# The order of plain score units between the other TensorE work in an attention stage

## The chip, the cores and the metric

The kernel runs on one core of a Trainium2 chip. The metric is device time of one execution in microseconds. Before the change the median of three runs is 2106.28 us (2105.14 to 2108.61).

## The reference

One transformer layer in fp32 over 2048 positions of width 512: x + attention(xn) + feed-forward(xn), where xn is x normalised over its last axis. Cut to what matters here:

```python
qkv = einsum('bsh,oh->bso', xn, w_qkv)      # 16 heads of 32
scores = einsum('bhqd,bhkd->bhqk', q, k) / sqrt(32)
scores = where(causal, scores, finfo.min)
probs = softmax(scores, axis=-1)
attn = einsum('bhqk,bhkd->bhqd', probs, v)
out = einsum('bsh,oh->bso', attn, w_o)
```

The feed-forward (512 to 4096 and back, weights unpacked from 4-bit codes) is not touched.

## The kernel before

There are three stages, each with one program for each engine and semaphores between them: norm_and_project, attention, project_and_feed_forward. The change is in the attention's TensorE program.

The attention computes each head's scores twice. The first time, the *plain score units* give the row maxima: `scores` (L628 to L638) multiplies 128 query rows by up to 512 keys into p_s, a PSUM tile with two buffers, and adds the causal mask to units on the diagonal with a second small matmul. VectorE's `unit_max` reduces each unit to one column of max_part (L533). A head has 40 units. They go through the query blocks 0 to 15 in order, each cut into chunks of 512 keys, so that the last unit of a block has 128, 256, 384 or 512 columns and a mask. `scores` waits until VectorE has reduced the unit two before (L629): maxed starts at 2.

`split_max` (L536 to L553) then splits a head's maxima into three bf16 parts. `turn_max` (L640 to L650) transposes them by matmul into p_o, ScalarE's `max_row` copies them into spare rows of q_stack, in four pieces of 512 columns a head.

The second time, `scores_t` (L652 to L668) computes transposed scores with the maximum already subtracted, in 20 *steps* a head. A step is 256 keys by 512 query columns (256 in the last step of each query chunk). The chunks have 2, 4, 6 and 8 steps; the last two of each carry masks. ScalarE takes the exponential (L490), and `product_v` (L670 to L683) multiplies it by v into p_o: two concurrent halves, which go to different partitions. At the end of a chunk ScalarE copies one half (`copy_half`), and VectorE's `add_halves` (L555 to L563, two operations of 512 columns) adds the halves and frees p_o.

TensorE's order is written out in `group` (L710 to L727), a loop over *pairs* of steps (d from 0 to 9). In a pair the transposed scores run two steps ahead of the products. The plain units of later heads are spread over the steps, two to each: BESIDE[s] (L294 to L297) holds units 10 to 39 of the next head in steps 0 to 14 and units 0 to 9 of the one after in steps 15 to 19. The order of a pair is: two units, scores_t of two steps, turn_max (pairs 8 and 9), two units, product_v of two steps, turn_max (pairs 8 and 9). The loop over groups of four heads jumps back twice; the last group is written out, and leaves out units of heads that don't exist.

VectorE's order is written in its own `group` (L601 to L617): for each step its two unit_max, and behind those of steps 3, 7 and 13 the add_halves of the chunk that ended two steps earlier; the last chunk's stands at the head's end. In step 15 split_max comes ahead of the units. Each engine takes its instructions in this order.

In the pairs the units have these columns (d for a mask): pair 0 512, 512d, 512, 512; pair 1 128d, 512, 512, 256d; pair 2 512, 512, 384d, 512; pair 3 512, 512d, 512, 512; pair 4 512, 128d, 512, 512; pair 5 512, 256d, 512, 512; pair 6 512, 384d, 512, 512; pair 7 512, 512d, 128d, 256d; pair 8 384d, 512d, 512, 128d; pair 9 512, 256d, 512, 384d..

Of the kernel before, what the change touches and what calls it, by code (L numbers as in the profile page):

```python
# [262 lines left out]
def attention(nc, qk_scratch, v_scratch, sum_scratch, rsum_scratch, wo_t, wo_sb, attn_t):  # L263
# [11 lines left out]
    GROUP = 4  # L275
# [3 lines left out]
    QK_BUFS = GROUP  # L279
# [3 lines left out]
    LEAD = 2  # L283
# [10 lines left out]
    BESIDE = {s: [] for s in range(NS)}  # L294
# [12 lines left out]
    with ExitStack() as ctx:  # L307
# [3 lines left out]
        def sem(name):  # L311
            return ctx.enter_context(nc.semaphore(name))
# [25 lines left out]
        qk_loaded = [sem(f"qk_loaded{i}") for i in range(QK_BUFS)]  # L338
# [107 lines left out]
        def ahead(g, j, s, steps, last):  # L446

            dj, s = divmod(s + steps, NS)
            if last and j + dj >= GROUP:
                return None  # L450
            return g * GROUP + j + dj, (j + dj) % GROUP, s
# [171 lines left out]
        @block.tensor  # L623
        def _(pe):
            pe.sem_inc(pv_done, E_BUFS)
            pe.wait_ge(consts, NC + 3)

            def scores(h, par, u):  # L628

                i, k, w = UNITS[u]  # L630
                diagonal = k + w == P * (i + 1)
                pe.wait_ge(maxed, h * NU + u + 1)
                last = nc.tensor.matmul(p_s[:, u % 2, 0:w], q_stack[par][0:ROWS, i * P:(i + 1) * P],  # L633
                                        k_stack[par][0:ROWS, k:k + w], start=True, stop=not diagonal)
                if diagonal:
                    last = nc.tensor.matmul(p_s[:, u % 2, w - P:w], ident[:, :], mask_q[:, :],
                                            start=False, stop=True)
                last.then_inc(scored, 1)  # L638

            def turn_max(h, r):  # L640

                if r == 0:
                    pe.wait_ge(max_split, h + 1)
                    pe.wait_ge(o_free, h * TC + 1)
                    pe.wait_ge(denom_made, h * TC + 1)
                pe.wait_ge(max_rows, h * TC + r + 1)
                for t in range(W // P):
                    last = nc.tensor.matmul(p_o[:, 0, t * P:(t + 1) * P], max_cols[:, r * (W // P) + t, :],
                                            ident[:, :], start=True, stop=True)
                last.then_inc(max_turned, 1)  # L650

            def scores_t(h, par, s):  # L652

                qc, pair, q0 = STEPS[s]
                w = W - q0
                if pair == 0:
                    pe.wait_ge(max_rows, h * TC + qc + 2)
                pe.wait_ge(exp_done, h * NS + s + 1)
                for t in range(2):
                    kt = 2 * pair + t  # L660
                    diagonal = kt * P >= qc * W
                    last = nc.tensor.matmul(p_st[:, s % 2, t, 0:w], k_stack[par][:, kt * P:(kt + 1) * P],  # L662
                                            q_stack[par][:, qc * W + q0:(qc + 1) * W], start=True,
                                            stop=not diagonal)
                    if diagonal:
                        last = nc.tensor.matmul(p_st[:, s % 2, t, 0:(t + 1) * P], ident[:, :],
                                                mask_k[:, (1 - t) * P:], start=False, stop=True)
                last.then_inc(st_ready, 1)  # L668

            def product_v(h, par, s):  # L670
                qc, pair, q0 = STEPS[s]
                w = W - q0
                if pair == 0:
                    pe.wait_ge(o_free, h * TC + qc + 1)
                    pe.wait_ge(denom_made, h * TC + qc + 1)
                if s == 0:
                    pe.wait_ge(max_rows, (h + 1) * TC + 1)
                pe.wait_ge(exp_done, h * NS + s + 3)
                for t in range(2):
                    last = nc.tensor.matmul(p_o[2 * t * D:2 * t * D + VW, qc % 2, q0:], v_stack[par][:, 2 * pair + t, :],  # L680
                                            e_sb[:, s % E_BUFS, t, 0:w], start=pair == 0, stop=s in LAST)
                last.then_inc(pv_done, 1)

            pe.sem_inc(maxed, 2)
            pe.sem_inc(max_rows, 1)
            for u in range(NU):
                if u == 0:
                    pe.wait_ge(qk_loaded[0], 96)
                scores(0, 0, u)
            for r in range(TC):  # L690
                turn_max(0, r)
            pe.wait_ge(minus_one, 2 * QK_BUFS + V_BUFS)
            for s in range(LEAD):
                scores_t(0, 0, s)
            for s in range(CHAIN, NS):
                for heads, u in BESIDE[s]:
                    if u == 0:
                        pe.wait_ge(qk_loaded[heads - 1], 96)
                    scores(heads - 1, heads - 1, u)

            def scores_beside(g, j, s, last):
                for heads, u in BESIDE[s]:
                    if last and j + heads >= GROUP:
                        continue
                    par = (j + heads) % QK_BUFS
                    if u == 0:
                        pe.wait_ge(qk_loaded[par], (g + (j + heads) // QK_BUFS + 1) * 96)
                    scores(g * GROUP + j + heads, par, u)

            def group(g, last):  # L710
                for j in range(GROUP):
                    h = g * GROUP + j
                    turns = not (last and j + 1 >= GROUP)
                    pe.wait_ge(v_loaded[j % V_BUFS], (g * (GROUP // V_BUFS) + j // V_BUFS + 1) * 16)
                    for d in range(ND):
                        s = 2 * d
                        scores_beside(g, j, s, last)
                        for n in (s, s + 1):
                            if (at := ahead(g, j, n, LEAD, last)) is not None:
                                scores_t(*at)  # L720
                        if turns and d >= ND - 2:
                            turn_max(h + 1, 2 * (d - ND + 2))
                        scores_beside(g, j, s + 1, last)
                        product_v(h, j % V_BUFS, s)
                        product_v(h, j % V_BUFS, s + 1)
                        if turns and d >= ND - 2:
                            turn_max(h + 1, 1 + 2 * (d - ND + 2))  # L727

            with pe.Fori(0, NH // GROUP - 1) as g:
                group(g, False)  # L730
            group(NH // GROUP - 1, True)


# [391 lines left out]
```

## Time and profile before

| | |
|---|---|
| median of 3 runs | 2106.28 us |
| profiled execution | 2107.61 us, span 2105.8 us, mean granted clock 0.969 |
| TensorE busy, matmuls | 1958.8 us (93%) |
| VectorE busy | 1197.6 us (57%) |
| ScalarE busy | 706.9 us (34%) |
| GpSimd busy | 239.1 us (11%) |
| attention | from about 200 to 944 us |
| feed-forward | from about 962 us to the end |

The span goes from the first to the last instruction of one profiled execution. An engine's busy time leaves out its waits. Matmuls are pipelined and their recorded ends are modelled, so that the record of one outlasts the start of the next. PEld stands for TensorE's weight loads, which run beside its matmuls. The granted clock is TensorE's: 1.00 is 2.4 GHz, 0.50 is 1.2 GHz. What is named behind "idle before" is what ended that idle time.

### The profile page before, as it was taken

To read this page: it belongs to the slowest core of one execution; us is meant where nothing else is said; L and a number is where in the kernel's file an instruction comes from. 1 tells how busy PE (TensorE), PEld (TensorE's weight loads), DVE (VectorE), ACT (ScalarE), POOL (GpSimd) and SP (SyncE) were. 2 spreads that over 40 slices of the span, in tenths; PEclk is the share of its full clock that TensorE was granted. 3 is DMA by queue.
4 is the path that set the end of the run, shared out by engine and by line. 5 is a ranking of instruction groups with operands and counts; after the bars stand their busy time and mean duration, and the time that the engine had idled before them with its cause. 6 is when DMAs were issued, how large, how long until landed. Compare 5 with 4: busy or idle time off the path is not lost.

```text
span 2105.8 us, 25238 instructions
## 1 busy us (share of the span) xinstructions
PE 1958.8 (93%) x8704; PEld 1337.9 (64%) x8704; DVE 1197.6 (57%) x1645; ACT 706.9 (34%) x825; POOL 239.1 (11%) x153
## 2 busy tenths in 40 slices
PE   2997899989999999987999999999999999999998
PEld 2885444444444444433777877788777877778776
DVE  7211666666667666665355655555655655656543
ACT  2221254544555545550123232222232222222221
POOL 0003000000000000000112122111122121111121
PEclk9998699999999999998999999999999999999999
DMA  3755211123111121305211011100110011110002
GB/s 140 247 173 145 65 36 36 36 39 67 37 37 36 36 56 23 68 20 191 60 31 31 0 30 30 30 23 7 30 30 30 0 30 30 30 27 3 0 1 80
DMA packets 84862, 106.29 MB, mean 50 GB/s; under 512 B 41680, under 2 KB 58256, under 8 KB 80976
## 3 DMA queue, kind: packets, MB, share of 16 engines
q1 hardware_dynamic: 84784, 105.27, 18.8%
q8 instruction: 47, 0.77, 0.2%
q14 instruction: 31, 0.25, 0.0%
HBM read 75.62 MB, written 29.61 MB: 50 GB/s over the span
## 4 chain that ended last, share of the span: by engine, by line
DVE 21%; ACT 11%; POOL 10%; issue 6%; PE 6%; POOLq 0%; DVEq 0%; ACTq 0%
POOL poly L923 7%; DVE acc L996 5%; DVE inter L976 4%; DVE inter L980 4%; ACT inter L895 3%; POOL poly L920 3%; ACT gate L891 3%; ACT poly L892 3%; DVE weight L965 3%; ACT i_hi L898 2%; DVE pair L952 2%; DVE magnitude L959 2%; PE p_out L1061 1%; DVE high L956 1%; DVE pair L950 1%
## 5 line engine op out<-in xcount | busy, mean ns | idle before, releaser
L533 DVE TENSOR_REDUCE max_part<-p_s 128x1 f32<-128x512 f32 (+3 forms) x640 | 364.2, 606 | 255.7 <-PE p_s L633 144.1
L490 ACT ACTIVATE e_sb<-p_st 128x1024 f32<-128x1024 f32 x320 | 282.8, 935 | 248.8 <-PE p_st L662 146.9
L680 PE MATMUL p_o<-e_sb,v_stack 128*33 128x512 f32 (+1 forms) x1280 | 292.1, 579 | 3.5 <-DVE acc L558 3.5
L633 PE MATMUL p_s<-k_stack,q_stack 96*128 96x512 f32 (+3 forms) x640 | 241.5, 445 | 50.2 <-DVE max_part L533 29.7
L976 DVE SCALAR_TENSOR_TENSOR inter<-inter,gate 128x1024 f32<-128x1024 f32 x64 | 78.4, 1226 | 329.4 <-ACT inter L895 329.4
L920 POOL TENSOR_SCALAR poly<-poly 128x1024 f32<-128x1024 f32 x64 | 67.4, 1053 | 1649.4 <-ACT poly L892 1649.4
L633 PEld LDWEIGHTS p_s<-k_stack,q_stack 96*128 96x128 f32 x640 | 115.4, 202 | 177.7 <-DVE max_part L533 131.7
L48 PE MATMUL p_up<-xn_hi,w_hi 128*128 128x512 f32 x512 | 201.0, 393 | 25.4 <-DVE inter L980 25.4
L48 PE MATMUL p_out<-i_hi,w_hi 128*128 128x512 f32 x512 | 200.0, 391 | 3.1 <-DVE acc L996 3.1
L48 PE MATMUL p_gate<-xn_hi,w_hi 128*128 128x512 f32 x512 | 201.5, 394 | 0.6 <-ACT poly L892 0.6
L662 PE MATMUL p_st<-q_stack,k_stack 128*128 128x512 f32 (+1 forms) x640 | 200.6, 422 | 0.0
L49 PE MATMUL p_out<-i_lo,w_hi 128*128 128x512 f32 x512 | 199.9, 391 | 0.0
L50 PE MATMUL p_out<-i_hi,w_lo 128*128 128x512 f32 x512 | 199.7, 390 | 0.0
L49 PE MATMUL p_gate<-xn_lo,w_hi 128*128 128x512 f32 x512 | 199.4, 389 | 0.0
L49 PE MATMUL p_up<-xn_lo,w_hi 128*128 128x512 f32 x512 | 199.4, 389 | 0.0
L50 PE MATMUL p_up<-xn_hi,w_lo 128*128 128x512 f32 x512 | 199.4, 389 | 0.0
L50 PE MATMUL p_gate<-xn_hi,w_lo 128*128 128x512 f32 x512 | 199.3, 389 | 0.0
L885 ACT ACTIVATE w_hi<-weight 128x1024 fp32r<-128x1024 f32 x48 | 50.9, 1061 | 393.1 <-DVE weight L965 393.1
L680 PEld LDWEIGHTS p_o<-e_sb,v_stack 128*33 128x33 f32 x1280 | 63.1, 113 | 143.9 <-issue 107.2
L923 POOL TENSOR_TENSOR poly<-poly,gate 128x1024 f32<-128x1024 f32 x64 | 153.2, 2393 | 5.3
L996 DVE TENSOR_TENSOR acc<-acc,p_out 128x2048 f32<-128x2048 f32 x64 | 145.9, 2280 | 7.5 <-PE p_out L50 7.5
L895 ACT ACTIVATE inter<-poly 128x1024 f32<-128x1024 f32 x64 | 67.9, 1061 | 240.5 <-POOL poly L923 240.5
(105 smaller groups left out, 2623.0 us busy)
## 6 DMA issues: line engine op xcount, KB each, us to landing
q_stack<-qk_scratch SPq DMA_DIRECT2D x48, 256.0 KB, 4.3
k_stack<-qk_scratch SPq DMA_DIRECT2D x48, 256.0 KB, 6.7
qk_scratch<-out_hi SPq DMA_DIRECT2D x32, 256.0 KB, 2.6
qk_scratch<-out_lo SPq DMA_DIRECT2D x32, 256.0 KB, 3.3
scales<-in_gate_up_s SPq DMA_DIRECT2D x128, 64.0 KB, 2.3
x_sb<-in_x SPq DMA_DIRECT2D x4, 1024.0 KB, 12.0
xn_lo_scratch<-xn_lo_made SPq DMA_DIRECT2D x1, 4096.0 KB, 13.3
v_scratch<-out_v SPq DMA_DIRECT2D x16, 256.0 KB, 2.0
```

The costliest lines, as they stand in the source:

```text
L48: nc.tensor.matmul(out, w_hi, x_hi, start=first, stop=False)
L49: nc.tensor.matmul(out, w_hi, x_lo, start=False, stop=False)
L50: return nc.tensor.matmul(out, w_lo, x_hi, start=False, stop=last)
L490: nc.scalar.activation(e_sb[:, s % E_BUFS, :, 0:w], p_st[:, s % 2, :, 0:w], ACT.Exp, scale=SCALE).then_inc(exp_done, 1)
L533: nc.vector.reduce_max(max_part[:, i, k // CAP:k // CAP + 1], p_s[:, u % 2, 0:w], AX.X).then_inc(maxed, 1)
L633: last = nc.tensor.matmul(p_s[:, u % 2, 0:w], q_stack[par][0:ROWS, i * P:(i + 1) * P], k_stack[par][0:ROWS, k:k + w], start=True, stop=not ...
L662: last = nc.tensor.matmul(p_st[:, s % 2, t, 0:w], k_stack[par][:, kt * P:(kt + 1) * P], q_stack[par][:, qc * W + q0:(qc + 1) * W], start=True,
L680: last = nc.tensor.matmul(p_o[2 * t * D:2 * t * D + VW, qc % 2, q0:], v_stack[par][:, 2 * pair + t, :], e_sb[:, s % E_BUFS, t, 0:w], start ...
L895: nc.scalar.activation(inter[:, :, :], poly[:, :, :], ACT.Tanh, scale=GELU_B).then_inc(tanh_done, 1)
L923: nc.gpsimd.tensor_tensor(poly[:, :, :], poly[:, :, :], gate[:, :, :], ALU.mult).then_inc(poly_done, 1)
L976: nc.vector.scalar_tensor_tensor(inter[:, :, :], inter[:, :, :], 1.0, gate[:, :, :], ALU.add, ALU.mult).then_inc(gelu_done, 1)
L996: nc.vector.tensor_tensor(here, here, p_out[:, :, :], ALU.add).then_inc(added, 1)
```

## The change

The four plain units of a pair no longer stand two by two. scores_beside places one unit, and is called four times in a pair. The new order of a pair is: unit, scores_t of one step, unit, scores_t of the other step, turn_max (pairs 8 and 9), unit, product_v of two steps, turn_max (pairs 8 and 9), unit. Only TensorE's program changes.

```diff
--- before.py
+++ after.py
@@ -698,14 +698,18 @@
                         pe.wait_ge(qk_loaded[heads - 1], 96)
                     scores(heads - 1, heads - 1, u)
 
-            def scores_beside(g, j, s, last):
-                for heads, u in BESIDE[s]:
-                    if last and j + heads >= GROUP:
-                        continue
-                    par = (j + heads) % QK_BUFS
-                    if u == 0:
-                        pe.wait_ge(qk_loaded[par], (g + (j + heads) // QK_BUFS + 1) * 96)
-                    scores(g * GROUP + j + heads, par, u)
+            def scores_beside(g, j, s, last, which):
+                heads, u = BESIDE[s][which]
+                if last and j + heads >= GROUP:
+                    return
+                par = (j + heads) % QK_BUFS
+                if u == 0:
+                    pe.wait_ge(qk_loaded[par], (g + (j + heads) // QK_BUFS + 1) * 96)
+                scores(g * GROUP + j + heads, par, u)
+
+            def scores_t_ahead(g, j, s, last):
+                if (at := ahead(g, j, s, LEAD, last)) is not None:
+                    scores_t(*at)
 
             def group(g, last):
                 for j in range(GROUP):
@@ -714,17 +718,18 @@
                     pe.wait_ge(v_loaded[j % V_BUFS], (g * (GROUP // V_BUFS) + j // V_BUFS + 1) * 16)
                     for d in range(ND):
                         s = 2 * d
-                        scores_beside(g, j, s, last)
-                        for n in (s, s + 1):
-                            if (at := ahead(g, j, n, LEAD, last)) is not None:
-                                scores_t(*at)
+                        scores_beside(g, j, s, last, 0)
+                        scores_t_ahead(g, j, s, last)
+                        scores_beside(g, j, s, last, 1)
+                        scores_t_ahead(g, j, s + 1, last)
                         if turns and d >= ND - 2:
                             turn_max(h + 1, 2 * (d - ND + 2))
-                        scores_beside(g, j, s + 1, last)
+                        scores_beside(g, j, s + 1, last, 0)
                         product_v(h, j % V_BUFS, s)
                         product_v(h, j % V_BUFS, s + 1)
                         if turns and d >= ND - 2:
                             turn_max(h + 1, 1 + 2 * (d - ND + 2))
+                        scores_beside(g, j, s + 1, last, 1)
 
             with pe.Fori(0, NH // GROUP - 1) as g:
                 group(g, False)
```

## Rows read from the trace of the kernel before

**Rows 1.** Busy time by stage: stretch, its length, each engine, granted clock, DMA.

```profile
250.00:944.00 694.00, 657.22 (x3218) 304.88 (x3214) 456.99 (x825) 350.33 (x439) 0.00 (x0) 0.96 0.20 40
```

**Rows 2.** Waits in the attention: who for whom, us in all, times, longest.

```profile
PEld p_s L633 <- DVE max_part L533: 116.3, 165, 2.4
...
PE p_s L633 <- DVE max_part L533: 26.0, 25, 2.0
```

**Rows 3.** Busy time by stage, head 7: pairs 1 to 5, 7 and 9.

```profile
566.09:570.17 4.08, 4.08 (x23) 1.90 (x23) 2.93 (x6) 2.10 (x3) 0.00 (x0) 1.00 1.00 204
570.17:573.92 3.75, 3.75 (x18) 1.90 (x18) 2.92 (x5) 1.94 (x2) 0.00 (x0) 1.00 0.58 56
573.92:578.08 4.16, 4.16 (x18) 1.75 (x18) 3.42 (x6) 2.53 (x3) 0.00 (x0) 1.00 0.00 0
578.08:582.22 4.14, 4.14 (x22) 1.83 (x22) 2.72 (x5) 1.51 (x2) 0.00 (x0) 1.00 0.00 0
582.22:585.71 3.49, 3.49 (x18) 1.75 (x18) 2.31 (x4) 1.94 (x2) 0.00 (x0) 1.00 0.00 0
...
589.73:594.05 4.32, 4.15 (x20) 1.94 (x20) 3.63 (x11) 1.94 (x2) 0.00 (x0) 1.00 0.01 2
...
598.60:602.84 4.24, 4.24 (x32) 2.38 (x32) 2.18 (x4) 2.69 (x4) 0.00 (x0) 1.00 0.00 0
```

**Rows 4.** Timeline of TensorE, head 7, pair 3: start, us, instructions, idle before.

```profile
572.42 1.49 PE L680 MATMUL p_o<-e_sb,v_stack 128*33 128x512 f32 x8
573.83 0.73 PE L633 MATMUL p_s<-k_stack,q_stack 96*128 96x512 f32 x2
...
574.45 1.17 PE L662 MATMUL p_st<-q_stack,k_stack 128*128 128x512 f32 x4
...
576.14 1.91 PE L680 MATMUL p_o<-e_sb,v_stack 128*33 128x512 f32 x8
```

**Rows 5.** Timeline of VectorE, head 7, pair 3.

```profile
574.37 1.29 DVE L533 TENSOR_REDUCE max_part<-p_s 128x1 f32<-128x512 f32 x2 [1.15 <-PE p_s L633]
...
577.21 0.69 DVE L558 TENSOR_TENSOR acc<-p_o,half_sum 32x512 f32 x1
...
578.65 0.89 DVE L533 TENSOR_REDUCE max_part<-p_s 128x1 f32<-128x512 f32 x2
```

**Rows 6.** Groups of VectorE in the attention: busy us, mean ns, idle before.

```profile
L533 DVE TENSOR_REDUCE max_part<-p_s 128x1 f32<-128x512 f32 x413 | 272.9, 687 | 141.0 <-PE p_s L633 135.7 <-PE p_s L636 3.4
...
L533 DVE TENSOR_REDUCE max_part<-p_s 128x1 f32<-128x256 f32 x58 | 24.0, 414 | 0.0
```

**Rows 7.** Timelines of VectorE and TensorE where heads 6 and 7 meet.

```profile
559.78 0.69 DVE L558 TENSOR_TENSOR acc<-p_o,half_sum 32x512 f32 x1 [2.18 <-ACT half_sum L497]
...
561.22 1.97 DVE L533 TENSOR_REDUCE max_part<-p_s 128x1 f32<-128x512 f32 x3
...
561.97 1.39 PE L633 MATMUL p_s<-k_stack,q_stack 96*128 96x512 f32 x2 [2.00 <-DVE max_part L533]
```

**Rows 8.** Timeline of the weight loads, head 7, pairs 2, 3 and 0.

```profile
571.99 0.19 PEld L633 LDWEIGHTS p_s<-k_stack,q_stack 96*128 96x128 f32 x1
...
575.71 0.19 PEld L633 LDWEIGHTS p_s<-k_stack,q_stack 96*128 96x128 f32 x1 [0.31 <-DVE max_part L533]
...
562.56 0.29 PEld L633 LDWEIGHTS p_s<-k_stack,q_stack 96*128 96x128 f32 x1 [0.41 <-DVE max_part L533]
```

**Rows 9.** Timeline of TensorE at a loop jump, between heads 3 and 4.

```profile
424.65 0.73 PE L633 MATMUL p_s<-k_stack,q_stack 96*128 96x512 f32 x2 [3.07 <-issue]
```

**Rows 10.** Busy time by stage, pairs 0 and 1 together, of heads 1 and 9.

```profile
287.08:299.14 12.06, 9.97 (x44) 4.54 (x43) 6.89 (x12) 5.12 (x7) 0.00 (x0) 0.86 0.61 138
...
648.21:658.70 10.49, 8.40 (x44) 3.84 (x44) 6.89 (x12) 5.13 (x7) 0.00 (x0) 1.00 0.57 133
```

**Rows 11.** Timeline of TensorE and busy time by stage in the feed-forward.

```profile
1152.86 0.50 PE L48 MATMUL p_up<-xn_hi,w_hi 128*128 128x512 f32 x1 [1.60 <-DVE inter L980]
...
1064.00:2027.00 963.00, 938.52 (x4108) 768.45 (x4106) 562.27 (x573) 270.64 (x271) 196.44 (x114) 1.00 0.08 21
```

## The prediction

> **What bounds the kernel now.** I read the stages first. In the attention's stretch TensorE (PE) is busy 657.2 of 694.0 us, VectorE (DVE) 457.0 and ScalarE 350.3 [rows 1]: TensorE sets the pace, and a stall there costs its full length. The change touches only TensorE's order in this stretch, so the rest of the program keeps its time.
>
> The waits come second. In this stretch weight loads of the plain score units wait on VectorE's row maxima 165 times, 116.3 us in all; the score matmuls themselves only 25 times, 26.0 us [rows 2]. Most waits of a load are thus covered by matmuls still streaming, and few reach the array. What they hang on is p_s, with two buffers: unit n can't start before VectorE has reduced unit n-2.
>
> Third, one head pair by pair (a pair is one d, two steps). I call the units of a pair U0 to U3, their reductions r0 to r3, the transposed scores T and T', the products V. Head 7's pairs 1 to 5, 7 and 9 take 4.08, 3.75, 4.16, 4.14, 3.49, 4.32 and 4.24 us at full clock [rows 3]. Pair 0, where the heads meet, is the exception, below.
>
> **The queue behind the change.** Before, a pair is U0 U1 T T' U2 U3 V. After, it is U0 T U1 T' U2 V U3. Nothing is added or removed: the same matmuls, loads and waits. But VectorE's order stays as written: r0 r1 r2 r3, and after steps 3, 7 and 13 the additions of a finished chunk (add_halves, two operations) stand between r3 of pair 1, 3, 6 and r0 of the next pair. Before, U3 ran ahead of the products, so r3 and the additions ran under them. After, U3 runs behind the products, so r3 and the additions begin only when the next pair's U0 is already through; r0 comes behind them, and U2 of that pair waits for r0.
>
> **Term 1, U2 behind the additions.** The pair's time from the end of the previous products:
> - The first unit behind the products starts at 573.83, and its reduction at 574.37, 0.46 us after the products' end at 573.91 (572.42 + 1.49) [rows 4, 5]. So r3 starts at 0.46 and, at 0.69 for 512 columns (687 ns on average), ends at 1.15; for U3 of 256 columns (pair 1) it takes 0.41 and, the unit being shorter, ends at 0.85 [rows 5, 6].
> - The additions and the gaps around them: from 577.21 to the next reduction at 578.65 is 1.44 us, plus 0.03 ahead of them [rows 5]. r0 thus starts at 2.62 and ends at 3.31 (pair 1's follower: 2.32, 3.01).
> - A waiting unit starts 0.06 after a reduction (561.22 + 0.69 = 561.91, and 561.97), its load some 0.01 earlier [rows 7]. So U2 loads at 3.36 (3.06).
> - From the load of the last unit ahead of the products to their end: 575.71 to 578.05 = 2.34 us, and 571.99 to 573.91 = 1.92 where half of the products are 256 wide [rows 4, 8].
> - Pair 4 becomes 3.36 + 2.34 = 5.70 against 4.14: +1.56. Pair 2 becomes 3.06 + 1.92 + 0.03 for a masked unit = 5.01 against 3.75: +1.26. Pair 7's U2 has 128 columns, some 0.10 less: 5.60 against 4.32: +1.28 [rows 3].
>
> Units stand beside heads 0 to 14; in head 14 pair 7 has no U2. The term: 15 x 1.26 + 15 x 1.56 + 14 x 1.28 = 18.9 + 23.4 + 17.9 = 60.2 us. What hid the additions until now was 1.9 us of products; that cover is gone. The bounds: nothing, if r0 weren't behind the additions, and 44 x 1.99 = 88 us, the length of the one stall of this kind that the trace has, where the heads meet [rows 7].
>
> **Term 2, the U1 that follows U3 closely.** U3, U0 and T now stand ahead of U1, and U1 needs r3: it loads at 1.20 at the earliest. Until U2's load come U1 (0.25) and T' (0.50: T and T' last from 574.45 to 575.45 [rows 4]), and from there it is 2.34: pair 3 takes 4.29, with the mask matmul of its U1 4.31, against 4.16 [rows 3]. Before, the U3 of this pair waited for r1 instead (its load at 575.71, 0.31 idle [rows 8]): the wait moves rather than goes. By the same sum, with each pair's own widths, pair 1 grows by 0.20, pair 3 by 0.15, pair 5 by 0.29 and pair 6 by 0.24; pair 9 shrinks by 0.16, as its masked U3 of 384 columns moves on and a short one comes, and pair 8 by 0.02. Together 15 x 0.88 - 14 x 0.18 = +10.7 us. The bounds: 0 where T covers r3 after all, 20 if every U1 waits 0.4.
>
> **Term 3, where the heads meet.** The last additions wait for ScalarE's copy (559.78, idle 2.18 us before), the next reduction starts at 561.22, and U2 stands still for 2.00 us; U3's load follows at 562.56, 0.60 behind, again for a reduction [rows 7, 8]. ScalarE's copy comes at the same time after the change, r0 too; U2 keeps its release, but U3 now stands behind the products. So 0.60 us go at each of the 12 boundaries that have units and no loop jump: -7.2 us. At the two loop jumps TensorE waits 3.07 us on its own issue and r0 is ready by then [rows 9]: nothing. The visible idle time before U2 shrinks from 2.00 to 1.74, as U3 and its masks fill 0.26.
>
> **Term 4, the clock.** Ten of these 12 boundaries are followed by a spell at the lower clock level (1.2 instead of 2.4 GHz): pairs 0 and 1 take 12.06 us at a mean clock of 0.86 against 10.49 where the clock stays [rows 10], so 1.6 us a spell. What precedes it is 2.00 us of idle [rows 7]. In the feed-forward TensorE idles 1.60 us at a time for VectorE's line L980, and the clock stays at 1.00 over 963 us [rows 11]. The idle of term 1's stalls starts when T' is through. U3 starts at -0.08; U3, U0, U1 take 0.25 each, T and T' 0.50 each, masks up to 0.3, and a record outlasts the next start by 0.17 (574.45 + 1.17 = 575.62) [rows 4]: 1.84 to 2.15. To 3.36 (pair 2: 3.06) these are 1.2 to 1.5 us, below 1.60: I take no new spell. The boundaries' 1.74 lies between the rows: I take half of the ten spells as gone, -8.0 us; the bounds are 0 and -16.
>
> The Trainium skill speaks against this, in its page "TensorE: Matmul & The Clock Gate", section "A second HAM failure mode: psum-queue depth-cycling": where the engine idles briefly and often between groups of matmuls over rotating PSUM buffers, its clock swings between the two levels, and throughput goes down by that. The feed-forward's rows don't bear it out; the heads' boundaries do. By the rule all 44 new stalls would be followed by a spell: the first rival.
>
> **Sum.** 60.2 + 10.7 - 7.2 - 8.0 = +55.7 us on the profiled execution's own 2107.6 (span 2105.8): 2163.3. The median before is 2106.3, 1.3 lower: I predict 2162 us, 2.6% slower.
>
> **Rivals.**
> 1. *Every new stall costs a spell too.* For it: the attention's stretch is less dense than the feed-forward (657.2 of 694.0 against 938.5 of 963.0 us busy), so a shorter idle may do [rows 1, 11]. Against: idle of 1.60 never did. 44 x 1.6 = 70 and the 8 of term 4 not gained: 2240. 15%; a part of the stalls (a third) gives 2193.
> 2. *Only term 1 and 3 show.* T covers r3, and all ten spells go: 60.2 - 7.2 - 16 = +37: 2143. For it: 0.4 us is within what loads wait today without the array idling [rows 2]. Against: pair 3's U3 waits in just this way and pays. 10%.
> 3. *Faster.* One mechanism: spacing. With a piece of other work between any two units, no unit of a pair waits for the reduction that just began; the 26.0 us of matmul waits [rows 2] and the ten spells, 16 us, would go: 2064. It decides at the U2 that follows the additions: if VectorE has r0 done when T' ends, it holds. It would need some 1.3 us of slack in VectorE's queue just where U3 now comes 2 us later. 4%.
> 4. *It does nothing*, the waits only change places: 2106. Term 2 shows that for the ordinary pairs; the additions' place speaks against it for the others. 3%.
>
> The forecast itself has 68%. Its own range is 2150 to 2175; the range to hold 8 in 10 reaches down to rival 2 and up past a third of rival 1: 2142 to 2205. About 0.2% (4 us) can be told from no change in this kernel. Faster 4%, same 3%, slower 93%.
>
> **What would show it.** In the profile after, the idle before the score matmuls caused by VectorE's reductions grows from 26 us by some 55, in about 44 more waits of 1.3 to 1.5 us; pairs 2, 4 and 7 of head 7 take 5.0, 5.7 and 5.6 us, the others change by less than 0.35; VectorE's additions start about 1.2 us after the products' end and not under them; fewer rows at 0.86 where heads meet. I am wrong if the stall before U2 is missing or much shorter than 1.2 us, or if pairs 2, 4 and 7 carry a clock below 1.00.

## The result and the profile after

The changed kernel takes 2170.18 us at the median (2168.28 to 2171.04, 4 runs) against 2107.45 for the kernel before in the same comparison: a ratio of 1.0296, interval 1.0278 to 1.0314. Forecast were 2162 us, range 2142 to 2205. The profiled execution has 2168.28 us and a span of 2166.5, 60.7 above the span before.

The instructions are the same in number (25238). What has grown is idle time. The waits first, in the attention's stretch, now 250 to 1001 us: the columns are those of [rows 2].

```profile
PEld p_s L633 <- DVE max_part L533: 129.0, 145, 2.0
...
PE p_s L633 <- DVE max_part L533: 71.1, 58, 1.5
```

The score matmuls wait 58 times and 71.1 us on VectorE's reductions, where it was 25 times and 26.0 [rows 2]. The 58 are the 44 stalls of term 1, 12 where heads meet and 2 others; the 25 were 12 of 1.9 to 2.0 us and 13 small ones. The growth is 45 us and not 55: the idle in a stall is 1.07 to 1.23 us and not 1.3 to 1.5, as T' ends later than I summed, and where heads meet the idle fell from 2.00 to 1.52 us. The loads' waits have become fewer, 145 for 165. So it isn't the number of waits that decides, but how many reach the array.

Head 7 pair by pair, the busy time by stage as in [rows 3], all ten pairs:

```profile
584.05:589.87 5.82, 4.30 (x23) 1.96 (x23) 3.91 (x6) 3.05 (x4) 0.00 (x0) 1.00 0.19 55
589.87:594.14 4.27, 4.27 (x22) 1.89 (x22) 2.27 (x4) 2.11 (x3) 0.00 (x0) 1.00 1.03 226
594.14:599.15 5.01, 3.82 (x19) 1.86 (x19) 3.65 (x6) 1.94 (x2) 0.00 (x0) 1.00 0.83 113
599.15:603.52 4.37, 4.29 (x18) 1.75 (x18) 2.67 (x4) 2.65 (x3) 0.00 (x0) 1.00 0.00 0
603.52:609.25 5.73, 4.50 (x22) 2.04 (x22) 3.65 (x6) 1.51 (x2) 0.00 (x0) 1.00 0.00 0
609.25:613.08 3.83, 3.74 (x18) 1.75 (x18) 2.35 (x4) 2.05 (x2) 0.00 (x0) 1.00 0.00 0
613.08:617.40 4.32, 4.23 (x18) 1.75 (x18) 2.54 (x4) 2.64 (x3) 0.00 (x0) 1.00 0.00 0
617.40:623.02 5.62, 4.47 (x19) 1.83 (x19) 4.76 (x12) 2.05 (x2) 0.00 (x0) 1.00 0.02 5
623.02:627.67 4.65, 4.65 (x29) 2.28 (x30) 2.27 (x4) 2.10 (x3) 0.00 (x0) 1.00 0.00 0
627.67:631.85 4.18, 4.18 (x32) 2.35 (x33) 2.10 (x4) 2.69 (x4) 0.00 (x0) 1.00 0.00 0
```

Pairs 2, 4 and 7 (third, fifth and eighth row) take 5.01, 5.73 and 5.62 us against 3.75, 4.14 and 4.32 [rows 3]; forecast were 5.0, 5.7 and 5.6. In pair 2 only 3.82 of the 5.01 us are busy. All ten rows have a clock of 1.00. Pair 0 took 8.00 us before, in the spell (558.09 to 566.09), and takes 5.82.

Pairs 3 and 4 on VectorE, answering to [rows 5]:

```profile
599.59 2.80 DVE L533 TENSOR_REDUCE max_part<-p_s 128x1 f32<-128x512 f32 x4 [1.29 <-PE p_s L633]
603.96 0.69 DVE L533 TENSOR_REDUCE max_part<-p_s 128x1 f32<-128x512 f32 x1 [1.58 <-PE p_s L633]
604.68 0.69 DVE L558 TENSOR_TENSOR acc<-p_o,half_sum 32x512 f32 x1
605.41 0.69 DVE L562 TENSOR_TENSOR denom<-p_o,half_sum 1x512 f32<-1x512 f32 x1
606.13 0.89 DVE L533 TENSOR_REDUCE max_part<-p_s 128x1 f32<-128x512 f32 x2
```

The products of pair 3 end at 603.50, r3 starts at 603.96 as forecast (0.46 behind), the additions at 604.68, and r0 at 606.13. Under the products of pair 3, from 602.4 to 603.96, VectorE now has nothing to do. TensorE in pair 4:

```profile
601.59 1.91 PE L680 MATMUL p_o<-e_sb,v_stack 128*33 128x512 f32 x8
603.43 0.73 PE L633 MATMUL p_s<-k_stack,q_stack 96*128 96x512 f32 x2
...
604.92 0.36 PE L662 MATMUL p_st<-q_stack,k_stack 128*128 128x256 f32 x1
...
606.87 0.51 PE L633 MATMUL p_s<-k_stack,q_stack 96*128 96x512 f32 x1 [1.23 <-DVE max_part L533]
607.31 1.91 PE L680 MATMUL p_o<-e_sb,v_stack 128*33 128x512 f32 x8
```

T' starts at 604.92. U2 starts at 606.87 after 1.23 us of idle, 0.05 behind the end of r0 (606.13 + 0.69 = 606.82).

### The profile page after: what moved, and what is told of

Same layout as the page of the kernel before. It is cut to its first block, busy times and chain, and to the rows that moved or that the text cites. A ratio compares the mean times of both kernels' runs of the same rounds, so it can differ in the third digit from the quotient of the medians.

```text
span 2166.5 us, 25238 instructions
## 1 busy us (share of the span) xinstructions
PE 1967.7 (91%) x8704; PEld 1333.7 (62%) x8704; DVE 1210.1 (56%) x1645; ACT 714.7 (33%) x825; POOL 239.2 (11%) x153
## 4 chain that ended last, share of the span: by engine, by line
DVE 20%; ACT 11%; POOL 10%; issue 6%; PE 6%; POOLq 0%; DVEq 0%; ACTq 0%
POOL poly L928 7%; DVE acc L1001 5%; DVE inter L981 3%; DVE inter L985 3%; ACT inter L900 3%; POOL poly L925 3%; ACT gate L896 3%; ACT poly L897 3%; DVE weight L970 3%; ACT i_hi L903 2%; DVE magnitude L964 1%; DVE pair L957 1%; PE p_out L1066 1%; DVE high L961 1%; PE p_gate L1066 1%
## 5 line engine op out<-in xcount | busy, mean ns | idle before, releaser
L533 DVE TENSOR_REDUCE max_part<-p_s 128x1 f32<-128x512 f32 (+3 forms) x640 | 376.7, 609 | 327.7 <-PE p_s L633 174.8
L490 ACT ACTIVATE e_sb<-p_st 128x1024 f32<-128x1024 f32 x320 | 290.1, 937 | 291.5 <-PE p_st L662 169.3
L633 PE MATMUL p_s<-k_stack,q_stack 96*128 96x512 f32 (+3 forms) x640 | 266.8, 455 | 99.6 <-DVE max_part L533 75.3
L680 PE MATMUL p_o<-e_sb,v_stack 128*33 128x512 f32 (+1 forms) x1280 | 283.7, 565 | 3.2 <-DVE acc L558 3.2
L633 PEld LDWEIGHTS p_s<-k_stack,q_stack 96*128 96x128 f32 x640 | 119.9, 199 | 252.4 <-DVE max_part L533 144.5
L662 PE MATMUL p_st<-q_stack,k_stack 128*128 128x512 f32 (+1 forms) x640 | 217.9, 415 | 0.0
```

Of the source, the lines that this page charges most:

```text
L490: nc.scalar.activation(e_sb[:, s % E_BUFS, :, 0:w], p_st[:, s % 2, :, 0:w], ACT.Exp, scale=SCALE).then_inc(exp_done, 1)
L533: nc.vector.reduce_max(max_part[:, i, k // CAP:k // CAP + 1], p_s[:, u % 2, 0:w], AX.X).then_inc(maxed, 1)
```

## The experiments

In all of them the letters are those of the prediction. The kernel before, run beside each comparison, had 2107.21 and 2107.9 us at the median. Times by pair are those of head 7; in the kernels before and after the change heads 1 to 11 agree with it to 0.03 us in pairs 2 to 9.

### The halves of the change, one at a time

U0 and U1 are spaced, and U3 stays ahead of the products:

```diff
-scores_beside(g, j, s + 1, last, 0)
-product_v(h, j % V_BUFS, s)
+scores_beside(g, j, s + 1, last, 0)
+scores_beside(g, j, s + 1, last, 1)
+product_v(h, j % V_BUFS, s)
 ...
-scores_beside(g, j, s + 1, last, 1)
```

> Only the first half of the change: U0 T U1 T' U2 U3 V; U3 stays ahead of the products. My theory (the cost is U3 behind the products, with the additions between its reduction and the next pair's): no stall behind the additions, the 44 waits of 1.1 to 1.2 us are missing; r1 comes some 0.07 us later for U3 in the pairs whose U1 has 512 columns; the boundaries stay as before with their 0.60 and their spells. Time: before plus 2 to 8 us, 2110 to 2115. The rival (units one by one are dearer as such, by the array's switching between plain and transposed units): half of the +61 us, some 2135.

Measured: 2115.41 us (2111.28 to 2120.53), ratio 1.0045 (1.0029 to 1.0061). The pairs behind the additions keep their old times. Busy time by stage, pairs 1, 3, 4 and 7 of head 7:

```profile
565.57:569.98 4.41, 4.34 (x23) 1.97 (x23) 3.28 (x6) 2.10 (x3) 0.00 (x0) 1.00 1.03 223
573.81:578.15 4.34, 4.30 (x18) 1.76 (x18) 3.69 (x6) 2.53 (x3) 0.00 (x0) 1.00 0.00 0
578.15:582.28 4.13, 4.13 (x22) 1.80 (x22) 2.64 (x5) 1.51 (x2) 0.00 (x0) 1.00 0.00 0
589.95:594.24 4.29, 4.16 (x20) 1.95 (x20) 3.62 (x11) 1.94 (x2) 0.00 (x0) 1.00 0.01 2
```

Pair 4 takes 4.13 and pair 7 4.29 us. The stalls are not there. Pair 3 takes 4.34 against 4.16, pair 1 4.41 against 4.08: U1 comes 0.5 to 0.7 us later than beside U0, r1 with it, and U3, still close behind, pays. The 8 us lie at the upper edge of what I gave (2 to 8) and are an eighth of the change's cost; the rival's 2135 is out. They are a net sum: in the profiled execution pairs 1 to 9 grew by 11 us over heads 0 to 14, spells left out, and four of the ten spells were missing.

The other half alone: U0 and U1 side by side, U3 behind the products.

```diff
 scores_beside(g, j, s, last, 0)
-scores_t_ahead(g, j, s, last)
 scores_beside(g, j, s, last, 1)
+scores_t_ahead(g, j, s, last)
 scores_t_ahead(g, j, s + 1, last)
```

> Only the second half of the change: U0 U1 T T' U2 V U3. My theory: the three stalls behind the additions are there in full (60 us), and U1, now only U0 behind U3, waits for r3 with nothing but U0 in between: its load at 1.20 us, with T and T' both still to come. By the sum from the ends of reductions pairs 1, 3, 5, 6, 8, 9 are 0.3 to 0.7 us longer than in the changed kernel, together 2.7 us a head, 40 us: about 2210 us. The rival (spacing is the dear part): 2140, the other half of the +61.

Measured: 2209.44 us, ratio 1.0492 (1.0473 to 1.0511). Busy time by stage, pairs 2, 3 and 4:

```profile
617.32:622.32 5.00, 4.02 (x19) 1.92 (x19) 3.66 (x6) 1.94 (x2) 0.00 (x0) 1.00 0.70 87
622.32:627.15 4.83, 4.28 (x18) 1.74 (x18) 2.67 (x4) 2.53 (x3) 0.00 (x0) 1.00 0.00 0
627.15:632.87 5.72, 4.66 (x22) 1.95 (x22) 3.66 (x6) 1.51 (x2) 0.00 (x0) 1.00 0.00 0
```

That is my theory's 2210, and not the rival's 2140. Pairs 2 and 4 stall as in the changed kernel (5.00, 5.72), and pair 3 takes 4.83 where that has 4.37. So with U3 behind the products the spacing of U0 and U1 is worth 39 us, and with U3 ahead of them it costs 8. The halves can't be added: +8 and +102 alone, +63 together.

### Where VectorE's additions stand

TensorE's order stays that of the change; only VectorE's moves. First the additions go between r2 and r3:

```diff
-for heads, u in BESIDE[s]:
+for n, (heads, u) in enumerate(BESIDE[s]):
     ...
-if s - 2 in LAST:
-    add_halves(g, h, j, STEPS[s - 2][0])
+    if n == 0 and s - 2 in LAST:
+        add_halves(g, h, j, STEPS[s - 2][0])
```

> TensorE's order as in the changed kernel; on VectorE the additions of a chunk stand between r2 and r3 instead of behind r3, so that they run under the products again. My theory: pairs 2, 4 and 7 fall from 5.00, 5.72 and 5.62 to about 3.5, 4.1 and 4.2 us, 66 us in all: 2100 to 2106, at or slightly below the kernel before, because the boundaries keep their gain. The rival (U3 behind the products is dear by itself, whatever VectorE's order): it stays above 2140.

Measured: 2105.74 us (12 runs), ratio 0.9995 (0.9986 to 1.0005): no difference from the kernel before, and 64 us below the changed one. VectorE's timeline in pairs 3 and 4, and then the busy time by stage of pairs 2, 4 and 7:

```profile
569.94 0.69 DVE L558 TENSOR_TENSOR acc<-p_o,half_sum 32x512 f32 x1
570.66 0.69 DVE L562 TENSOR_TENSOR denom<-p_o,half_sum 1x512 f32<-1x512 f32 x1
571.48 1.49 DVE L533 TENSOR_REDUCE max_part<-p_s 128x1 f32<-128x512 f32 x3
```

```profile
563.13:566.67 3.54, 3.54 (x19) 1.85 (x19) 2.58 (x5) 1.94 (x2) 0.00 (x0) 1.00 0.75 70
571.04:575.27 4.23, 4.23 (x22) 1.96 (x22) 2.49 (x5) 1.51 (x2) 0.00 (x0) 1.00 0.00 0
583.45:587.72 4.27, 4.19 (x19) 1.84 (x19) 3.69 (x11) 2.05 (x2) 0.00 (x0) 1.00 0.03 6
```

The additions now start at 569.94, under the products that end at 571.02, and pairs 2, 4 and 7 take 3.54, 4.23 and 4.27 us. Over all heads these three pairs give back 63 us; the others keep the times of the changed kernel. This is the strongest evidence: nothing on TensorE has changed against the slow kernel. That the time draws level with the kernel before is a balance, of what the other pairs cost more and what the shorter waits where heads meet save.

Then one place later than in the changed kernel, between r0 and r1 (the condition is n == 0 and s - 3 in LAST):

> TensorE's order as in the changed kernel; on VectorE the additions stand one place later, between r0 and r1 of the next pair. My theory (only r0 behind the additions is dear): U2 of pairs 2, 4 and 7 finds r0 at 1.75 us and doesn't stall; r1 ends about 3.8, needed by U3 only behind the products at about 4.1; 2103 to 2112. The rival (the additions need the products' cover, anywhere else they cost 1.44 us each time, 44 x 1.44 = 63 us): about 2165.

Measured: 2129.81 us, ratio 1.0103 (1.0086 to 1.0121), outside what either theory gave. Pairs 2 and 4 are mended (3.54, 4.23). Pair 8 is not. VectorE's timeline from pair 7 on, TensorE's, and the busy time by stage of pairs 3 and 8:

```profile
598.61 0.69 DVE L558 TENSOR_TENSOR acc<-p_o,half_sum 32x512 f32 x1
...
600.05 0.69 DVE L533 TENSOR_REDUCE max_part<-p_s 128x1 f32<-128x512 f32 x1
...
602.15 0.62 DVE L533 TENSOR_REDUCE max_part<-p_s 128x1 f32<-128x128 f32 x2
```

```profile
602.50 0.44 PE L633 MATMUL p_s<-k_stack,q_stack 96*128 96x384 f32 x1 [1.01 <-DVE max_part L533]
```

```profile
579.88:584.46 4.58, 4.47 (x18) 1.85 (x18) 3.19 (x6) 2.55 (x3) 0.00 (x0) 1.00 0.03 4
601.13:607.01 5.88, 4.87 (x29) 2.35 (x30) 3.45 (x10) 2.10 (x3) 0.00 (x0) 1.00 0.00 0
```

Ahead of pair 7's r2 now stand the additions, r1 and split_max. r2 starts at 602.15, and U0 of pair 8, which needs its buffer, starts at 602.50 after 1.01 us of idle. Pair 8 takes 5.88 us for 4.65. In pair 3 a smaller wait of this kind shows (4.58 for 4.37). Moved work needs slack for every unit that the new place delays. I had looked at r0 and r1 only.

### The heads' boundaries, and a faster kernel

TensorE's order of the kernel before; the last chunk's additions of a head go behind r3 of the next head's pair 0:

```diff
 if s - 2 in LAST:
     add_halves(g, h, j, STEPS[s - 2][0])
-add_halves(g, h, j, TC - 1)
+        if s == 1 and j > 0:
+            add_halves(g, h - 1, j - 1, TC - 1)
+if j == GROUP - 1:
+    add_halves(g, h, j, TC - 1)
```

> TensorE's order of the kernel before; on VectorE the last chunk's additions of a head stand behind r3 of the next head's pair 0 instead of ahead of its r0, for all heads but the last of a group. My theory (a stall is r0 behind additions, here too, and the spell follows the stall): the 2.0 us and 0.60 us waits go at 11 boundaries with units, pair 0 falls from 6.35 to about 3.95 us, and with the idle goes the spell: 11 x 2.4 + 9 x 1.6 = 40 us: 2062 to 2072. The rival (the wait at the boundary is for ScalarE's turned maxima and copies, and moves to the products): 2100 to 2107.

Measured: 2069.37 us (2067.54 to 2071.41), ratio 0.9816 (0.9803 to 0.983), faster than both kernels and within what my theory gave; the rival's 2100 is out. Pairs 0 and 1, and then pair 0 in the kernel before, of heads 7 (in a spell) and 9:

```profile
537.67:541.57 3.90, 3.90 (x22) 1.93 (x21) 3.01 (x5) 3.02 (x4) 0.00 (x0) 1.00 0.00 0
541.57:545.86 4.29, 4.29 (x23) 1.99 (x23) 3.99 (x8) 2.10 (x3) 0.00 (x0) 1.00 0.41 100
```

```profile
558.09:566.09 8.00, 5.91 (x22) 2.22 (x22) 4.04 (x6) 3.02 (x4) 0.00 (x0) 0.79 0.43 102
648.21:654.61 6.40, 4.31 (x22) 1.93 (x22) 3.95 (x6) 3.02 (x4) 0.00 (x0) 1.00 0.31 78
```

Pair 0 takes 3.90 us at full clock where it took 8.00, or 6.40 without a spell.

The same with the changed TensorE order, all additions between r2 and r3:

> TensorE's order as in the changed kernel; all additions between r2 and r3, and the last chunk's in the next head's pair 0. My theory: as with the additions ahead of r3 alone (2106), less 11 boundaries of some 1.6 us and the spells left there (5 x 1.6): 2078 to 2090, behind the kernel before with its boundary mended by the price of U1 behind U3, 17 us. A rival (one by one is the better order once VectorE's is right): below 2065.

Measured: 2087.42 us, ratio 0.9903 (0.9888 to 0.9918), as my theory had it and 18 us above the kernel just shown. With VectorE's additions moved for either, one by one remains the dearer order.

Last, U3 between the products of the two steps. VectorE's order is that of the run just shown, and the edit is against that run:

```diff
 product_v(h, j % V_BUFS, s)
+scores_beside(g, j, s + 1, last, 1)
 product_v(h, j % V_BUFS, s + 1)
 ...
-scores_beside(g, j, s + 1, last, 1)
```

> The order U0 T U1 T' U2 V U3 V', U3 between the products of the two steps, with all additions between r2 and r3, the last chunk's in the next head's pair 0. My theory: r3 has half of the products as cover, so U1 no longer waits for it, and nothing waits for the additions: pair 3 about 4.1 us, pair 5 3.5, pair 6 4.0, pair 2 3.6: 2055 to 2068, some 5 us below the kernel before with its boundary mended. The rival: each piece more between products costs about 0.1 us in loads and fills, and it ends level with that kernel or above it, to 2080.

Measured: 2109.73 us, ratio 1.0006 (0.9997 to 1.0015). My theory fell, and by more than its rival allowed. TensorE's timeline in pair 3, and the busy time by stage of pairs 3 and 4:

```profile
572.18 1.05 PE L683 MATMUL p_o<-e_sb,v_stack 128*33 128x512 f32 x4
573.16 0.49 PE L636 MATMUL p_s<-k_stack,q_stack 96*128 96x512 f32 x1
573.59 1.05 PE L683 MATMUL p_o<-e_sb,v_stack 128*33 128x512 f32 x4
574.57 0.51 PE L636 MATMUL p_s<-k_stack,q_stack 96*128 96x512 f32 x1
```

```profile
570.31:574.66 4.35, 4.35 (x18) 1.66 (x18) 3.81 (x7) 2.53 (x3) 0.00 (x0) 1.00 0.63 59
574.66:579.12 4.46, 4.46 (x22) 1.79 (x22) 2.82 (x5) 1.51 (x2) 0.00 (x0) 1.00 0.00 0
```

No wait shows in these rows, so U1 indeed no longer waits for r3. But pair 4 takes 4.46 us for 4.14. In pair 3 U3 and the products of both steps last from 572.18 to 574.57, 2.39 us. In the changed kernel the products of both steps last 1.84 us in one piece (601.59 to 603.43). Here each step's take 0.98, 0.12 more for the two, and U3 takes 0.43, where a unit in the forecast's sum had 0.25: 0.3 us a pair for the place between the products.

Against the run before, where U3's place is the only difference, pairs 2, 4, 8 and 9 are longer by 0.28, 0.22, 0.23 and 0.38 us; in pairs 3, 5 and 6 the wait that is gone just pays for it (0.01 to 0.03 shorter), and pair 7 is 0.07 shorter. Together with pairs 0 and 1 that makes 22 us over heads 0 to 14, of which longer spells ahead of heads 4, 8 and 12, where the additions still stand at a group's end, are about 7. With the 18 us by which that run lies above the kernel with its boundary mended, this takes back the 38 us that mending the boundary brought. The theory saw what is saved and put the place between the products at nothing.

### Longer stalls: what the clock does

The changed kernel, with one more VectorE operation between the additions of chunks 0 to 2:

```diff
 nc.vector.tensor_tensor(attn_t[...], p_o[...], half_sum[...], ALU.add)
+if qc < TC - 1:
+    nc.vector.tensor_tensor(idle_work, half_sum[...], half_sum[...], ALU.add)
 nc.vector.tensor_tensor(denom[...], p_o[...], half_sum[...], ALU.add)
```

> The changed kernel, with one more VectorE operation of 512 columns (half_sum added to itself into an unused tile) between the two additions of chunks 0 to 2; the output doesn't depend on it. My theory: each of the 44 stalls is longer by 0.72 us, 31.7 us in all, and the idle in them is 1.8 to 1.95 us. If the clock falls after idle of that length, as it did where heads met, most of the 44 are followed by a spell of 1.6 us: up to 70 us more, 2240 to 2270. The rival (the spells at the boundaries are due to what surrounds them, not to the idle's length): plus 32 only, 2202, and no row below 1.00 in pairs 2, 4 and 7.

Measured: 2226.67 us, ratio 1.0559 (1.054 to 1.0578), 56.5 above the changed kernel and between the two theories (2240 and up; 2202). The operation and its gap take 0.70 us on VectorE, 44 times, 30.8 us. The rest goes with the clock. Busy time by stage of head 7's pairs 2, 4 and 7, and TensorE's timeline in pair 7:

```profile
620.79:626.81 6.02, 4.12 (x19) 1.84 (x19) 4.34 (x7) 1.94 (x2) 0.00 (x0) 0.93 0.68 96
632.05:640.10 8.05, 6.13 (x22) 2.22 (x22) 4.34 (x7) 1.51 (x2) 0.00 (x0) 0.79 0.00 0
648.26:655.68 7.42, 5.57 (x19) 1.90 (x19) 5.45 (x13) 2.05 (x2) 0.00 (x0) 0.84 0.00 0
```

```profile
652.31 0.33 PE L636 MATMUL p_s<-k_stack,q_stack 96*128 96x128 f32 x1 [1.78 <-DVE max_part L534]
...
652.64 3.02 PE L683 MATMUL p_o<-e_sb,v_stack 128*33 128x512 f32 x8
```

After idle of 1.78 us the products take 3.02 us for 1.91, and the mean clock of this pair is 0.84. Of the 44 stalls 21 are followed by a spell. In the two profiled executions pairs 2 to 9 of heads 0 to 14 grew by 61.4 us (head 13's pair 3 left out, where a spell went); less 30.8 that is 30.6, or 1.5 us a spell. Both theories had a part: length does bring spells, but at 1.65 to 1.92 us only to about half of the stalls. Counted in one profiled execution of each kernel, idle of the array in the attention and spells at the lower clock behind it:

| kernel and place | idle, us | spells |
|---|---|---|
| additions behind r0, pair 8 | 1.00 to 1.02 | 0 of 12 |
| second half, boundaries | 0.95 to 1.07, behind one of some 0.4 | 1 of 12 |
| changed, pairs 2, 4 and 7 | 1.07 to 1.23 | 0 of 44 |
| head 13's pair 3, in four of the kernels | 1.23 to 1.25 | 2 of 4 |
| changed, boundaries | 1.41 to 1.53 | 1 of 12 |
| additions ahead of r3, boundaries | 1.41 to 1.53 | 2 of 12 |
| additions behind r0, boundaries | 1.41 to 1.53 | 5 of 12 |
| longer stalls, boundaries | 1.41 to 1.53 | 0 of 12 |
| longer stalls, pairs 2, 4 and 7 | 1.65 to 1.92 | 21 of 44 |
| first half, boundaries | 1.87 to 1.99 | 6 of 12 |
| before, boundaries | 1.89 to 2.00 | 10 of 12 |

The counts belong to these executions and not to the kernels. The twelve executions of the kernel with the additions ahead of r3 go from 2103.1 us at a mean granted clock of 0.977 to 2109.4 us at 0.973, so some of them had more or longer spells than the one counted (2103.8 us). A difference of a few spells between two rows shows nothing; that of 0 of 44 against 21 of 44 does.

## Why the prediction was right, step by step

**Term 1** (60.2 us) is right in place and size. Over heads 0 to 14 pairs 2, 4 and 7, measured from end of products to end of products, grew by 18.6, 23.9 and 18.9 us, together 61.4. That the additions are the cause is shown by the run that has them ahead of r3: with that alone 64 us come back.

**Term 2** (10.7 us) was undersized: 16.9 us. The growth of pairs 1, 3, 5, 6, 8 and 9 is 0.19, 0.22, 0.36, 0.30, 0.10 and -0.06 us a head; forecast were 0.20, 0.15, 0.29, 0.24, -0.02 and -0.16. It isn't a wait that was missed: pair 8 is busy for 4.65 of its 4.65 us and yet 0.10 longer. The sum gave each unit 0.25 us and T' 0.50 wherever they stand. In the traces (medians of the time from a start to the next) a unit of 512 columns takes 0.23 us behind another unit or a transposed score, 0.32 behind a mask's matmul and 0.34 behind the products, and T' behind a masked U1 takes 0.55. In pair 8 the unit of 128 columns that now stands behind the turned maxima takes 0.15 us for 0.07. Placed one by one, more pieces stand behind one of another kind; why that costs is not shown. The wait for r3 is there as forecast: in pair 3 the array idles for the 0.08 us between 4.37 and 4.29 busy, the rest lies under modelled ends. The half that leaves U0 and U1 together shows it larger.

**Term 3** (-7.2 us) is right: the pairs 0 without a spell before, of heads 9 and 14, shrank by 0.58 and 0.59 us, which makes -7.0 for 12. The idle is 1.52 us and not 1.74: r0 comes at its old time, and T' ends 0.2 us later than the sum had it, by the same prices as in term 2.

**Term 4** (-8.0 us) had the right sign: of the ten spells one is left in the profiled execution, worth some 14 us and not 8: pairs 0 and 1 of all heads shrank by 17.6 us together, in which are -7.0 of term 3, +2.9 of pair 1 and +1.1 at the loop jumps. The half was a choice between two rows and not a mechanism, and with the same idle at the boundaries the runs above had 0 to 5 spells left, so neither number should be leaned on. No spell follows a stall of pairs 2, 4 or 7, so the first rival is out for this kernel. It was nearer than I gave it, though: 0.6 to 0.7 us more of idle brings a spell to half of the stalls, and head 13's idle of 1.24 us (below) has one. The rule of the Trainium skill, "TensorE: Matmul & The Clock Gate", section "A second HAM failure mode: psum-queue depth-cycling", that short idle times between groups of matmuls make the clock swing, thus agrees with the boundaries and with the longer stalls (21 spells in 44), and not with the change's own stalls (0 in 44).

**Not foreseen:** in head 13 a reciprocal of 1.75 us (the inverted sums) stands ahead of pair 3's r0, and U3 behind the products made this a stall as well. VectorE's timeline and TensorE's:

```profile
890.58 1.75 DVE L577 RECIPROCAL recip<-recip 96x256 f32<-96x256 f32 x1
```

```profile
892.93 0.49 PE L633 MATMUL p_s<-k_stack,q_stack 96*128 96x512 f32 x1 [1.24 <-DVE max_part L533]
893.36 3.39 PE L680 MATMUL p_o<-e_sb,v_stack 128*33 128x512 f32 x8
```

The pair takes 7.35 us for 4.62 (clock 0.79), +2.7, and a spell follows its 1.24 us of idle. What lies behind head 14 nearly cancels: head 15 ends its own work 3.0 us sooner, but the wait for the last chunk's sums is 2.5 us longer, and the first projections run 1.2 us longer at the lower clock.

**The sum** is nearer than its terms. The profiled span grew by 60.7 us where 55.7 were forecast. Term 2 was 6 us too small and head 13 (+2.7) was not in it, but term 4 saved 6 to 7 us more than forecast: these misses nearly cancel, and that is luck. What carries the forecast is term 1.

**The rivals.** "Only terms 1 and 3" (2143) fell with term 2, and "it does nothing" (2106) with the 44 stalls. "Faster" was right in its premise, that a unit between two other pieces seldom waits, and wrong at the point that it named itself: r0 isn't done when T' ends. With the additions ahead of r3 it is, and even then the order only draws level.

## What to carry to other kernels

When work moves in one engine's queue, write the consumer's queue beside it and ask what stands there between the moved item's result and the next one waited for. Here two additions of 1.44 us, harmless under the products, made a pair 1.24 to 1.59 us longer, 44 times, without being touched. Before changing the busiest engine's order, move the small work in the other queue: this alone gave 38 us here, with TensorE's order as it was.

## What the runs showed of the hardware

Whether idle is followed by a spell at the lower clock does not hang on its length alone. At the same place of the same instruction order on TensorE, idle of 1.41 to 1.53 us was followed by a spell 0, 1, 2 and 5 times of 12, in one execution each of four kernels that differ only in VectorE's program. In the denser feed-forward 16 idle times of 1.56 to 1.60 us had none [rows 11], and in the attention one of 1.24 us had one. What decides between them was not tested. Length has its part: 0.6 to 0.7 us more in the same 44 stalls took the spells from 0 to 21.

A matmul's price hangs on what stands before it. A unit of 96 rows by 512 columns takes 0.23 us behind its like and 0.34 behind the fp32 products; placed between two steps' products it takes 0.43 and makes the products 0.12 longer, although no wait shows. The cause was not tested.
